# A transformer block with self- and cross-attention: the attention loop's instruction orders rewritten on five engines, and two tiles of cross keys placed by one group of transfers

## The chip, the cores and the metric

One core of a Trainium2 chip. The metric is the time of one execution on the device in microseconds (us), the median of several runs.

## What is computed

A batch of B = 32 items of N = 100 rows with D = 320 features passes a self-attention, a cross-attention to 361 context rows of 192 features, and a gated feed-forward layer, all in float32; both attentions have 20 heads of 16 features. Cut to what matters:

```python
def _attn(x, ctx, wq, wk, wv, wo, bo, heads):
    q, k, v = (heads_of(x @ wq), heads_of(ctx @ wk), heads_of(ctx @ wv))
    a = softmax(einsum('bhid,bhjd->bhij', q, k) * dh ** -0.5)
    return merge(einsum('bhij,bhjd->bhid', a, v)) @ wo + bo
h1 = _ln(x, n1_g, n1_b); x = _attn(h1, h1, q1, k1, v1, o1_w, o1_b, 20) + x
h2 = _ln(x, n2_g, n2_b); x = _attn(h2, context, q2, k2, v2, o2_w, o2_b, 20) + x
h3 = _ln(x, n3_g, n3_b); a, g = split(h3 @ ff_w1 + ff_b1)
return a * gelu(g) @ ff_w2 + ff_b2 + x
```

## The kernel before, in words

Three stages follow each other. A first stage makes the queries, keys and values of self-attention for all items and stores them in DRAM. The attention stage (`attention_phase`) is what the change touches. The feed-forward stage comes last.

The attention stage is a software pipeline without a loop in the program: for each engine an order of calls is written out by hand, `lead_in()`, 29 times `period(x, s, c, f)`, `run_out()`. In period p the roles are x = p, s = p + 1, c = p + 2, f = p + 3. Item f has its own (self-attention) scores made for their maximum, c goes through self-attention's exponentials and products, its output projection, the second norm, and the projections for cross-attention; s has its cross scores made for their maximum; x goes through cross-attention's exponentials and value products; y = x − 1 gets its cross output projection and its result. Every engine runs its calls strictly in the order written, and semaphores order the engines among each other. A call that has to wait holds back all calls behind it on its engine.

The steps, with the lines of the profile:

- `self_scores(f, i)` on TensorE (L167), two halves of ten matmuls, and `cross_scores(s, c)` (L785), ten pairs of matmuls of 362 columns, all write one PSUM tensor of two banks, `score`. So each of these twelve products waits (`empty_score`) until VectorE's `maximum` of the one before it (L174 for own, L1095 for cross scores) is done.
- `turn_max` (L796, job "MT1" or "MT2") transposes the finished maxima; ScalarE's `max_high` (L1392) and VectorE's `max_low` (L1111) split them into two parts of lower precision, and SyncE's `place_max` (L160) writes these into the query stack `qs`, as additional rows, so that the second product of queries and keys comes out with the maximum subtracted.
- `scores_for_exp` on TensorE (L811) makes that second product, two matmuls of 200 columns a tile, into two buffers `expin`; ScalarE's `exponential` (L1414) turns it into `probs`. There are 5 tiles for self-attention and 15 for cross-attention a period. `times_v` (L833) multiplies them with the values.
- `copy_product` (ScalarE, L181 and L183), `turn_heads` (VectorE, a transpose L1140 and a reciprocal L195), `scale_products` (GpSimd, L190), `turn_back` (VectorE, L1149), `heads_high` (ScalarE, L1435) and `heads_low` (GpSimd, L1628) bring the product into the form that `project_out` (TensorE, L702 and L705, eight matmuls) reads.
- `second_input` (VectorE, L1157) adds the residual, takes the statistics (L1161, L1164), and `normalise` (L1171) follows after GpSimd's `inverse_deviation`. `turn_normalised` (L684), `project_q2` (L702, L705) and `turn_q2` (L721) make the cross queries, which `copy_q2` and `q2_high` (ScalarE) and `q2_low` (VectorE) prepare. SyncE's `place_q2` (L566) writes them in six transfers into the stack, which GpSimd's `clear_cross` (L1603) has set to zero once the last exponent product of two items before has read it.
- `project_kc(c, t)` (L732 to L736, five matmuls, three tiles of keys) and `project_vc(c, i)` (L747 to L751, five matmuls, three tiles of values) project the context, which GpSimd splits into `ctx_hi` and `ctx_lo` (`split_first`, `split_last`, L1645 and L1646). `kc_high` (ScalarE, L1383) and `kc_low` (VectorE, L1111) prepare each key tile, and SyncE's `place_kc` (L548) writes it into the key stack `ks` in three transfers.
- All projections and transposes use three PSUM banks in turn, in the order of the list `WORK`: job number i goes to bank i mod 3, and waits until the job three before it has been read. `EXP` and `PV` number the exponentials and value products in the same way.

The seam of two periods on TensorE is this:

```python
cross_scores(s, 9)
turn_max(2, s)          # end of a period
self_scores(f, 0)       # next period, with the next f
```

Here `turn_max(2, s)` waits for the maximum of the pair just made.

## Time and profile before

| | us |
|---|---|
| median of 3 runs | 1479.38 |
| lowest, highest | 1477.76, 1483.56 |
| profiled execution | 1477.44 |
| its span, first to last instruction | 1475.5 |
| TensorE (matmuls) busy | 1317.4 |
| VectorE, ScalarE, GpSimd busy | 821.9, 675.6, 602.1 |
| mean granted clock of TensorE | 0.959 of full speed |

How to read the rows below: in a timeline a row gives start, duration, engine, line, operation, output and inputs, shapes and the number of instructions merged into it; in brackets stands the idle time just before it and what ended that. The modelled durations of successive matmuls overlap, so the time that a step takes of TensorE is read from its start to the next start. In a table of stretches a row gives the stretch and its length, then busy time and number of instructions for TensorE (matmuls), its weight loads, VectorE, ScalarE and GpSimd, then the granted clock (1.00 is 2.4 GHz, 0.50 is 1.2 GHz), the DMA share and GB/s. SPq is SyncE's queue; its durations are those of issuing transfers.

### The profile page before, as it was taken

How to read it: one execution, taken by the hardware profiler on the slowest of the kernel's cores; microseconds unless marked ns; L12 is line 12 of the kernel's file. 1: busy time of each engine (PE TensorE's matmuls, PEld its weight loads, DVE VectorE, ACT ScalarE, POOL GpSimd, SP SyncE). 2: the span in 40 equal slices, each digit the busy share in tenths (PEclk: the TensorE clock that was granted, in tenths of full speed). 3: DMA queues.
4: the chain of work that ended last, by engine and by line, in shares of the span. 5: the costliest groups of instructions: out<-in, count | busy, mean ns of one | idle time of the engine just before them, and what ended most of it. 6: DMA issues, size and time to landing. Idle time of an engine off the chain costs nothing. (4 is left out here: it accounts for less than half of the span.)

```text
span 1475.5 us, 34459 instructions
## 1 busy us (share of the span) xinstructions
PE 1317.4 (89%) x12788; PEld 1192.6 (81%) x12788; DVE 821.9 (56%) x1606; ACT 675.6 (46%) x1622; POOL 602.1 (41%) x792
## 2 busy tenths in 40 slices
PE   6898789988988898989889888988877999999999
PEld 5898678777777777777777777777657999999999
DVE  5464565766666666666666666667554524242421
ACT  5564244554555455455545554555444332323231
POOL 6331333444344444444443444344226533333341
PEclk9999889999999999999999999999888999999999
DMA  4677533443434444344434433342211110101000
GB/s 127 207 253 236 162 105 120 127 122 107 129 117 128 126 137 151 111 137 145 135 107 121 130 112 114 122 131 85 77 41 59 33 37 14 32 13 31 18 6 23
DMA packets 119691, 154.52 MB, mean 105 GB/s; under 512 B 23036, under 2 KB 113396, under 8 KB 119540
## 3 DMA queue, kind: packets, MB, share of 16 engines
q1 hardware_dynamic: 119540, 152.50, 33.5%
q8 instruction: 96, 1.57, 0.4%
q14 instruction: 55, 0.45, 0.1%
HBM read 62.98 MB, written 28.93 MB: 62 GB/s over the span
## 5 line engine op out<-in xcount | busy, mean ns | idle before, releaser
L1414 ACT ACTIVATE probs<-expin 120x400 f32<-120x400 f32 (+2 forms) x635 | 293.7, 504 | 242.9 <-PE expin L811 228.3
L1095 DVE TENSOR_REDUCE neg_max<-score 100x2 f32<-100x722 f32 x320 | 284.8, 890 | 78.6 <-PE score L785 78.6
L811 PE MATMUL expin<-qs,ks 128*120 128x200 f32 (+2 forms) x1270 | 233.7, 292 | 11.1 <-ACT probs L1414 8.9
L811 PEld LDWEIGHTS expin<-qs,ks 128*120 128x120 f32 (+2 forms) x1270 | 186.5, 189 | 49.8 <-ACT probs L1414 34.7
L785 PE MATMUL score<-ks,qs 128*100 128x362 f32 x640 | 172.8, 351 | 58.0 <-DVE neg_max L1095 55.1
L190 POOL TENSOR_TENSOR scaled_heads<-turned_heads,rden 128x320 f32<-128x320 f32 x63 | 47.7, 758 | 366.8 <-DVE rden L195 366.8
L785 PEld LDWEIGHTS score<-ks,qs 128*100 128x100 f32 x640 | 82.4, 166 | 97.1 <-issue 64.6
L2638 DVE SCALAR_TENSOR_TENSOR hidden<-ps_a,b_cols,gelu 128x320 f32<-128x320 f32 x100 | 55.0, 550 | 175.1 <-PE ps_a L2562 175.0
L174 DVE TENSOR_REDUCE neg_max<-score 100x10 f32<-100x1000 f32 x62 | 74.4, 1200 | 131.6 <-PE score L167 131.6
L2800 POOL TENSOR_TENSOR hid_lo<-hidden,hid_hi 128x320 fp32r<-128x320 f32 x100 | 88.0, 880 | 122.4 <-ACT hid_hi L2708 122.2
L1603 POOL MEMSET qs<- 128x2400 f32 (+1 forms) x58 | 112.6, 1941 | 32.9 <-PE expin L811 32.9
L2720 ACT ACTIVATE gelu<-ps_g,b_cols 128x320 f32<-128x320 f32 x100 | 52.8, 528 | 138.1 <-PE ps_g L2562 138.1
L2562 PE MATMUL ps_g<-t_hi,w_hi 128*128 128x320 f32 x300 | 92.6, 314 | 10.1 <-DVEq L2477 10.1
L833 PE MATMUL attn<-probs,vc 120*17 120x100 f32 (+1 forms) x3840 | 97.3, 251 | 0.1
L1111 DVE TENSOR_TENSOR kc_parts<-work,kc_parts 128x362 fp32r<-128x362 f32 (+1 forms) x96 | 51.0, 531 | 74.2 <-ACT kc_parts L1383 74.2
L2562 PE MATMUL ps_g<-t_hi,w_lo 128*128 128x320 f32 x300 | 91.8, 311 | 0.0
L2562 PE MATMUL ps_a<-t_hi,w_lo 128*128 128x320 f32 x300 | 91.6, 310 | 0.0
L2562 PE MATMUL ps_a<-t_hi,w_hi 128*128 128x320 f32 x300 | 91.5, 310 | 0.0
L833 PEld LDWEIGHTS attn<-probs,vc 120*17 120x17 f32 (+1 forms) x3840 | 80.8, 97 | 8.7 <-ACT probs L1414 1.1
L1628 POOL TENSOR_TENSOR t_lo_OT<-dense_heads,t_hi_OT 128x300 fp32r<-128x300 f32 x63 | 52.0, 825 | 77.1 <-ACT t_hi_OT L1435 77.1
L2579 PE MATMUL ps_y<-w_hi,hid_hi 128*128 128x320 f32 x250 | 78.5, 314 | 0.0
L2580 PE MATMUL ps_y<-w_lo,hid_hi 128*128 128x320 f32 x250 | 77.1, 309 | 0.0
(222 smaller groups left out, 3050.9 us busy)
## 6 DMA issues: line engine op xcount, KB each, us to landing
ks<-kc_parts SPq DMA_DIRECT2D x192, 181.0 KB, 2.7
qk_dram<-qk_parts SPq DMA_DIRECT2D x32, 500.0 KB, 5.3
qs<-q_parts SPq DMA_DIRECT2D x192, 75.0 KB
ks<-qk_dram SPq DMA_DIRECT2D x96, 125.0 KB
ctx_raw<-in_ctxT SPq DMA_DIRECT2D x64, 180.5 KB
ks<-kc_parts SPq DMA_DIRECT2D x96, 90.5 KB, 2.2
qs<-qk_dram SPq DMA_DIRECT2D x64, 125.0 KB
v_dram<-v_rows SPq DMA_DIRECT2D x32, 132.8 KB
```

The costliest lines, as they stand in the source:

```text
L174: return nc.vector.tensor_reduce(neg_max[:, :, n * i:n * (i + 1)], src, AX_X, ALU.max, negate=True)
L785: mm = pe.matmul(score[0:N, a, 0:JP], qs[2][u][:, a, q_slot(c), :], ks[2][u][:, c, :], start=True, stop=True)
L811: mm = pe.matmul(dst, ks[a][u][:, c, j0:j0 + n], qs[a][u][:, :, q_slot(c) if a == 2 else c, :], start=True, stop=True)
L833: mm = pe.matmul(attn[32 * i:32 * i + D1, g * N:(g + 1) * N], v, probs[EXP_AT[a, b, g, jt] % NPT][0:n, i * N:(i + 1) * N], start=(jt == 0) ...
L1095: ins = nc.vector.tensor_reduce(dst, src, AX_X, ALU.max, negate=True)
L1414: nc.scalar.activation(probs[e % NPT][0:n, :], expin[e % 2][0:n, 0:HG * N], ACT.Exp, scale=SCALE)\
L1603: link(nc.gpsimd.memset(stack.rearrange("p a c n -> p (a c n)").bitcast(F32), 0.0))
L2562: mm = pe.matmul(bank[:, 0:W], a, b, start=(k == 0), stop=(k == len(passes) - 1))
L2579: pe.matmul(y, hid_hi[:, f, c], w2_hi[:, f, :], start=(f == 0), stop=False)
L2580: pe.matmul(y, hid_hi[:, f, c], w2_lo[:, f, :], start=False, stop=False)
L2638: nc.vector.scalar_tensor_tensor(out=hidden[n % 2][:], in0=ps_a[n % 2][:, 0:W], scalar=b1[:, n % FT:n % FT + 1], in1=gelu[n % 2][:], op0=A ...
L2800: nc.gpsimd.tensor_tensor(hid_lo[:, f, c], hidden[n % 2][:], hid_hi[:, f, c].bitcast(F32), ALU.subtract).then_inc(hid_lo_made, 1)
```

## The change

It gives every engine a new order of calls in the attention stage, for the period, the lead-in and the run-out. The products still share one score buffer. Of the seam, `turn_max(2, ·)` moves into the next period, `project_vc(c, 0)` and `project_vc(c, 1)` move to the period's end, `project_vc(s, 2)` to the next period. The first exponent tile of an item's self-attention moves to the end of the period before. SyncE's `place_q2`, `place_max(2, ·)` and the placing of key tile 2 move over the seam as well, and so do GpSimd's context split, VectorE's `turn_back(2, ·)`, and others. `second_input` is parted into the residual and `statistics(b)`. Key tiles 0 and 1 are placed by one group of three transfers with rows twice as long, which needs another order of the ten key slots (`k_slot`); a period has six key transfers where it had nine. The lists `WORK` and `EXP` follow. The diff of the periods, of what they call, and of `work_jobs` and `exp_jobs`; the lead-in and the run-out follow the same new orders and are left out, apart from `project_out(2, 30)`, which in the run-out now stands between `turn_max(2, 31)` and `scores_for_exp(2, 31, 0, 0)`, and `project_out(1, 0)`, which comes after `self_scores(1, 0)`, `self_scores(1, 1)`, `turn_max(1, 1)` and two key projections; `load_qkv1(2)` is issued after `place_max(1, 1)` there.

```diff
 def work_jobs(x, s, c, f):
     y = None if x is None or x == 0 else x - 1
-    order = [("KC", c, 0), ("O2", y, 0), ("MT1", f, 0), ("KC", c, 1), ("O1", c, 0), ("KC", c, 2), ("VC", c, 0),
-             ("T2", c, 0), ("Q2", c, 0), ("VC", c, 1), ("QT", c, 0), ("VC", c, 2), ("MT2", s, 0)]
+    order = [("MT2", x, 0), ("VC", s, 2), ("O2", y, 0), ("MT1", f, 0), ("KC", c, 0), ("KC", c, 1), ("O1", c, 0),
+             ("T2", c, 0), ("KC", c, 2), ("Q2", c, 0), ("QT", c, 0), ("VC", c, 0), ("VC", c, 1)]
     return [job for job in order if job[1] is not None]
...
 def exp_jobs(x, s, c, f):
-    order = [(1, c, 0, 0), (1, c, 1, 0), (1, c, 2, 0), (1, c, 3, 0), (1, c, 4, 0), (2, x, 0, 0), (2, x, 0, 1),
-             (2, x, 0, 2), (2, x, 1, 0), (2, x, 1, 1), (2, x, 1, 2), (2, x, 2, 0), (2, x, 2, 1), (2, x, 2, 2),
-             (2, x, 3, 0), (2, x, 3, 1), (2, x, 3, 2), (2, x, 4, 0), (2, x, 4, 1), (2, x, 4, 2)]
+    order = [(1, c, 1, 0), (1, c, 2, 0), (1, c, 3, 0), (1, c, 4, 0), (2, x, 0, 0), (2, x, 0, 1), (2, x, 0, 2),
+             (2, x, 1, 0), (2, x, 1, 1), (2, x, 1, 2), (2, x, 2, 0), (2, x, 2, 1), (2, x, 2, 2), (2, x, 3, 0),
+             (2, x, 3, 1), (2, x, 3, 2), (2, x, 4, 0), (2, x, 4, 1), (2, x, 4, 2), (1, f, 0, 0)]
     return [job for job in order if job[1] is not None]
...
+
+
+def k_slot(c):
+    return 2 * (c % 4) + c // 4 if c < 8 else c
...
     def place_kc(b, t):
         u = b % 2
-        sp.wait_ge(*emptied(("KC", b, t)))
-        cross_stack_free(b, min(2 * t + 1, G - 1))
-        c0, n = KT[t]
+        for i in (0, 1) if t == 0 else (2,):
+            sp.wait_ge(*emptied(("KC", b, i)))
+        cross_stack_free(b, 3 if t == 0 else G - 1)
+        c0, n, tiles = (0, 8, slice(0, 2)) if t == 0 else (8, 2, slice(2, 3))
         for slot, part in ((0, 0), (1, 0), (2, 1)):
             sp.dma_start(ks[2][u][product_rows(slot), c0:c0 + n, :].bitcast(F32),
-                         kc_parts[0:32 * n, part, t, :].bitcast(F32)).then_inc(kc_landed[t][u], 16)
+                         kc_parts[0:32 * KT[t][1], part, tiles, :].bitcast(F32)).then_inc(kc_landed[t][u], 16)
...
     def period(x, s, c, f, e):
         y = x - 1 if x else None
-        load_x(f)
+        v = y - 1 if y else None
+        place_q2(s)
+        place_max(2, x)
         load_context(f)
-        place_kc(c, 0)
-        store_x2(y)
+        place_kc(s, 2)
+        load_x(e)
         place_max(1, f)
         load_qkv1(e)
-        place_q2(c)
-        place_max(2, s)
-        place_kc(c, 2)
-        place_kc(c, 1)
+        store_x2(v)
+        place_kc(c, 0)
...
-        if c % 4 == 0:
+        if c in (0, 8):
...
-            mm = pe.matmul(score[0:N, a, 0:JP], qs[2][u][:, a, q_slot(c), :], ks[2][u][:, c, :],
+            mm = pe.matmul(score[0:N, a, 0:JP], qs[2][u][:, a, q_slot(c), :], ks[2][u][:, k_slot(c), :],
...
     def period(x, s, c, f):
         y = x - 1 if x else None
         self_scores(f, 0)
-        scores_for_exp(1, c, 0, 0)
         scores_for_exp(1, c, 1, 0)
-        project_kc(c, 0)
         scores_for_exp(1, c, 2, 0)
+        turn_max(2, x)
+        project_vc(s, 2)
         scores_for_exp(1, c, 3, 0)
-        project_out(2, y)
+        scores_for_exp(1, c, 4, 0)
         self_scores(f, 1)
-        scores_for_exp(1, c, 4, 0)
         times_v(1, c, 0)
         times_v(1, c, 1)
         times_v(1, c, 2)
         times_v(1, c, 3)
         times_v(1, c, 4)
+        cross_scores(s, 0)
+        project_out(2, y)
+        turn_max(1, f)
         scores_for_exp(2, x, 0, 0)
-        cross_scores(s, 0)
+        cross_scores(s, 1)
         scores_for_exp(2, x, 0, 1)
-        turn_max(1, f)
+        project_kc(c, 0)
         scores_for_exp(2, x, 0, 2)
         scores_for_exp(2, x, 1, 0)
-        cross_scores(s, 1)
-        scores_for_exp(2, x, 1, 1)
-        times_v(2, x, 0)
-        scores_for_exp(2, x, 1, 2)
-        scores_for_exp(2, x, 2, 0)
         cross_scores(s, 2)
         project_kc(c, 1)
-        scores_for_exp(2, x, 2, 1)
-        scores_for_exp(2, x, 2, 2)
+        scores_for_exp(2, x, 1, 1)
+        scores_for_exp(2, x, 1, 2)
         cross_scores(s, 3)
         project_out(1, c)
+        scores_for_exp(2, x, 2, 0)
+        scores_for_exp(2, x, 2, 1)
+        cross_scores(s, 4)
+        times_v(2, x, 0)
+        scores_for_exp(2, x, 2, 2)
         scores_for_exp(2, x, 3, 0)
+        times_v(2, x, 1)
+        cross_scores(s, 5)
         scores_for_exp(2, x, 3, 1)
+        scores_for_exp(2, x, 3, 2)
+        turn_normalised(c)
         project_kc(c, 2)
-        cross_scores(s, 4)
-        scores_for_exp(2, x, 3, 2)
+        cross_scores(s, 6)
         scores_for_exp(2, x, 4, 0)
-        project_vc(c, 0)
+        project_q2(c)
+        cross_scores(s, 7)
         scores_for_exp(2, x, 4, 1)
-        cross_scores(s, 5)
         scores_for_exp(2, x, 4, 2)
-        turn_normalised(c)
-        times_v(2, x, 1)
         times_v(2, x, 2)
+        turn_q2(c)
+        cross_scores(s, 8)
+        scores_for_exp(1, f, 0, 0)
         times_v(2, x, 3)
         times_v(2, x, 4)
-        cross_scores(s, 6)
-        project_q2(c)
-        cross_scores(s, 7)
+        cross_scores(s, 9)
+        project_vc(c, 0)
         project_vc(c, 1)
-        turn_q2(c)
-        cross_scores(s, 8)
-        project_vc(c, 2)
-        cross_scores(s, 9)
-        turn_max(2, s)
...
-    def statistics():
+    def statistics(b):
+        dve.wait_ge(*emptied(("O1", b, 0)))
...
     def period(x, s, c, f):
         y = x - 1 if x else None
         maximum(1, f, 0)
+        max_low(2, x)
+        turn_back(2, y)
         maximum(1, f, 1)
-        kc_low(c, 0)
-        result(y)
         maximum(2, s, 0)
         turn_heads(1, c)
         maximum(2, s, 1)
-        max_low(1, f)
+        result(y)
         turn_back(1, c)
         maximum(2, s, 2)
+        max_low(1, f)
+        kc_low(c, 0)
         kc_low(c, 1)
+        maximum(2, s, 3)
         second_input(c)
-        maximum(2, s, 3)
+        statistics(c)
+        maximum(2, s, 4)
         normalise(c)
-        maximum(2, s, 4)
         maximum(2, s, 5)
         features_low("T2", c)
+        maximum(2, s, 6)
         kc_low(c, 2)
-        maximum(2, s, 6)
-        turn_heads(2, x)
         maximum(2, s, 7)
         maximum(2, s, 8)
         q2_low(c)
-        turn_back(2, x)
         maximum(2, s, 9)
-        max_low(2, s)
+        turn_heads(2, x)
     nc.vector.memset(attn[:, :], 0.0).then_inc(attn_cleared, 1)
...
     def period(x, s, c, f):
-        exponential(1, c, 0, 0)
+        y = x - 1 if x else None
+        copy_vc(s, 1)
+        copy_vc(s, 0)
         exponential(1, c, 1, 0)
         exponential(1, c, 2, 0)
+        max_high(2, x)
         exponential(1, c, 3, 0)
         exponential(1, c, 4, 0)
-        kc_high(c, 0)
+        heads_high(2, y)
+        copy_vc(s, 2)
         copy_product(1, c)
+        max_high(1, f)
         exponential(2, x, 0, 0)
         exponential(2, x, 0, 1)
-        max_high(1, f)
+        kc_high(c, 0)
         exponential(2, x, 0, 2)
         exponential(2, x, 1, 0)
+        heads_high(1, c)
+        kc_high(c, 1)
         exponential(2, x, 1, 1)
-        heads_high(1, c)
         exponential(2, x, 1, 2)
         exponential(2, x, 2, 0)
         exponential(2, x, 2, 1)
         exponential(2, x, 2, 2)
-        kc_high(c, 1)
         exponential(2, x, 3, 0)
         exponential(2, x, 3, 1)
+        features_high("T2", c)
         exponential(2, x, 3, 2)
+        kc_high(c, 2)
         exponential(2, x, 4, 0)
+        copy_q2(c)
         exponential(2, x, 4, 1)
-        features_high("T2", c)
         exponential(2, x, 4, 2)
-        kc_high(c, 2)
+        exponential(1, f, 0, 0)
+        q2_high(c)
         copy_product(2, x)
-        copy_vc(c, 0)
-        copy_q2(c)
-        copy_vc(c, 1)
-        q2_high(c)
-        heads_high(2, x)
-        max_high(2, s)
-        copy_vc(c, 2)
...
     lead_in()
     for p in PERIODS:
         x, s, c, f = roles(p)
+        y = x - 1 if x else None
+        e = p + 4 if p + 4 < B else None
+        scale_products(2, y)
+        split_first(c)
+        heads_low(2, y)
+        split_last(c)
         scale_products(1, c)
+        clear_own(e)
         heads_low(1, c)
-        clear_own(p + 4 if p + 4 < B else None)
         inverse_deviation(c)
         second_residual(c)
-        first_residual(f)
+        first_residual(e)
         clear_cross(c)
-        scale_products(2, x)
-        split_first(f)
-        heads_low(2, x)
-        split_last(f)
```

## Rows read from the trace of the kernel before

**Rows 1.** The page's busy times, TensorE, and its DMA issues, key transfers.
```profile
PE 1317.4 (89%) x12788; PEld 1192.6 (81%) x12788; DVE 821.9 (56%) x1606; ACT 675.6 (46%) x1622; POOL 602.1 (41%) x792
...
ks<-kc_parts SPq DMA_DIRECT2D x192, 181.0 KB, 2.7
```

**Rows 2.** Stretches: lead-in, loop, run-out, then two single periods of the loop.
```profile
150.29:192.24 41.95, 32.79 (x218) 27.33 (x218) 24.67 (x45) 11.72 (x30) 14.35 (x21) 0.87 0.51 156
...
192.24:1032.94 840.70, 744.45 (x8750) 648.48 (x8750) 552.27 (x927) 441.67 (x1101) 371.66 (x403) 0.96 0.40 122
...
1032.94:1104.80 71.86, 58.12 (x636) 47.20 (x636) 37.55 (x74) 33.04 (x79) 15.55 (x24) 0.85 0.22 60
...
540.28:568.40 28.12, 24.73 (x302) 21.41 (x303) 19.05 (x32) 15.23 (x38) 12.94 (x15) 1.00 0.45 137
...
568.40:598.06 29.66, 26.25 (x302) 22.93 (x303) 19.05 (x32) 15.24 (x38) 12.93 (x15) 0.94 0.42 130
```

**Rows 3.** Timeline of TensorE, one period at full clock: instructions that waited, waits in brackets.
```profile
542.27 0.41 PE L732 MATMUL work<-ctx_hi,w_c 128*128 128x362 f32 x1 [0.40 <-POOL ctx_lo L1646]
...
556.63 0.55 PE L785 MATMUL score<-ks,qs 128*100 128x362 f32 x2 [1.05 <-DVE neg_max L1095]
...
565.18 0.54 PE L785 MATMUL score<-ks,qs 128*100 128x362 f32 x2 [0.34 <-DVE neg_max L1095]
...
566.73 0.58 PE L785 MATMUL score<-ks,qs 128*100 128x362 f32 x2 [0.26 <-DVE neg_max L1095]
...
568.40 0.25 PE L796 MATMUL work<-identf,neg_max 100*24 100x100 f32 x1 [1.10 <-DVE neg_max L1095]
```

**Rows 4.** Timeline of TensorE, the same period: slots from start to start.
```profile
544.72 1.00 PE L167 MATMUL score<-ks,qs 128*100 128x100 f32 x10
...
545.56 0.39 PE L811 MATMUL expin<-qs,ks 128*100 128x200 f32 x2
...
545.87 1.05 PE L833 MATMUL attn<-probs,vs 100*17 100x100 f32 x40
...
546.86 0.46 PE L811 MATMUL expin<-qs,ks 128*120 128x200 f32 x2
...
547.15 0.50 PE L785 MATMUL score<-ks,qs 128*100 128x362 f32 x2
...
563.68 0.31 PE L747 MATMUL work<-w_c,ctx_hi 128*120 128x320 f32 x1
...
564.41 0.42 PE L721 MATMUL work<-identf,q_rows 100*128 100x100 f32 x3
```

**Rows 5.** Timeline of VectorE, the same period: a maximum of own scores, one of cross scores.
```profile
545.76 1.20 DVE L174 TENSOR_REDUCE neg_max<-score 100x10 f32<-100x1000 f32 x1 [3.06 <-PE score L167]
...
565.76 0.91 DVE L1095 TENSOR_REDUCE neg_max<-score 100x2 f32<-100x722 f32 x1 [0.72 <-PE score L785]
```

**Rows 6.** Stretches around the seam of two periods, and around a mid-period wait.
```profile
565.00:570.30 5.30, 3.45 (x24) 2.71 (x24) 3.46 (x7) 1.79 (x7) 4.35 (x6) 1.00 0.26 87
...
570.30:574.00 3.70, 3.62 (x15) 3.63 (x16) 0.53 (x1) 1.35 (x4) 0.00 (x0) 0.54 0.27 58
...
555.00:558.00 3.00, 1.95 (x14) 1.60 (x13) 2.74 (x6) 1.07 (x4) 2.15 (x4) 1.00 0.41 128
```

**Rows 7.** Timelines of the run-out: TensorE twice, GpSimd, SyncE's queue.
```profile
1053.82 0.46 PE L811 MATMUL expin<-qs,ks 128*121 128x200 f32 x2
...
1062.92 0.90 PE L785 MATMUL score<-ks,qs 128*100 128x362 f32 x2 [2.41 <-issue]
...
1054.34 2.10 POOL L1603 MEMSET qs<- 128x2400 f32 x1 [4.50 <-PE expin L811]
...
1056.58 4.84 SPq L566 DMA_DIRECT2D qs<-q_parts  x6
```

**Rows 8.** Timeline of TensorE, end of the run-out: maxima turned, first exponent product.
```profile
1081.10 0.25 PE L796 MATMUL work<-identf,neg_max 100*24 100x100 f32 x1
...
1084.89 0.67 PE L811 MATMUL expin<-qs,ks 128*120 128x200 f32 x4 [2.12 <-DMA qs<-max_parts]
```

More of the change, by code:

```diff
@@ L917, in run_out @@
                 cross_scores(30, 0)
+                project_out(2, 28)
                 scores_for_exp(2, 29, 0, 0)
@@ L1238, in lead_in @@
                 maximum(2, 0, 1)
+                turn_back(1, 1)
+                maximum(2, 0, 2)
+                max_low(1, 2)
+                kc_low(1, 0)
                 kc_low(1, 1)
-                maximum(2, 0, 2)
-                turn_back(1, 1)
                 maximum(2, 0, 3)
                 second_input(1)
+                statistics(1)
                 maximum(2, 0, 4)
```

282 lines of the change are left out of this document (144 added, 138 removed), and 17 rows, old and new, of tables (DRAIN_EXP, FILL_WORK).

## The prediction

> **What bounds the kernel now.** Read the page first: TensorE is busy 89% of the span, far ahead of every other engine [rows 1]. Then cut the span by stage [rows 2]: the 29 loop periods take 840.70 us of the 1475.5, at a mean granted clock of 0.96. So a period costs 28.99 us on average, but the one quoted at full clock took 28.12, and the next, with the same 302 matmuls, 29.66 at 0.94. Two losses follow. TensorE works 24.73 of the 28.12 us, so 3.4 us of every period is waiting; and the clock adds 840.70 − 29 × 28.12 = 25.2 us over the loop. VectorE works 19.05 us of a period, ScalarE 15.23: neither could set the end alone.
>
> The waits [rows 3] name their cause: 1.10, 1.05, 0.34 and 0.26 us for VectorE's maximum, because one score buffer serves all twelve score products, and 0.40 us for GpSimd's `ctx_lo`, which gates the first key projection. The 1.10 stands at the seam: `turn_max(2, s)` asks for the maximum of the product issued just before it, and the next period's `self_scores` sits behind it. Another small wait, for an exponential, makes up the rest.
>
> The clock falls at that seam. In the stretch before the fall the engine was busy 3.45 of 5.30 us, with the waits of 0.34, 0.26, 1.10 and 0.40 in it; then the clock was 0.54 (nearly all at its lower level, 1.2 GHz) for 3.7 us. Around the lone 1.05 wait in mid-period it stayed 1.00 [rows 6].
>
> **The change, part by part.** No instruction of TensorE, VectorE, ScalarE or GpSimd is added or dropped in a period; the order changes, so work is 24.73 us as before and only waits and clock can move. I walk TensorE's new order against VectorE's, with slots (start to next start) at full clock [rows 4]: half of the own scores 0.84, one exponent tile 0.30, five own value products 0.99, a value projection 0.73. That is 0.146 per matmul of 320 columns, so a projection of eight takes 1.17, a key projection (five of 362 columns) 0.83, a cross score pair (two of 362) 0.33, taken as 0.38; a cross value product of 24 I take as 0.6. The score buffer's cost [rows 5]: own scores from 544.72, maximum at 545.76 for 1.20, next score at 547.15, that is 1.04 + 1.20 + 0.19 = 2.43 start to start; cross pair 565.18, maximum 565.76 for 0.91, next pair 566.73, 1.55 to 1.6 start to start. Anything VectorE does in between adds if it lies in its way.
>
> *Seam.* Now `cross_scores(s, 9)` is followed by two value projections (1.46 us), and `turn_max(2, ·)` waits until after two exponent products of the next period. The maximum needs 1.6 us from the pair's start, the pair and the projections cover 1.85: the 1.10 goes. What is late next is `turn_heads(2, x)`, which now ends VectorE's period: 0.83 plus 0.3 behind that maximum, until about 0.6 us after the period's start, but the own scores' maximum can't start before 1.07. Covered.
>
> *Own scores.* Between the halves stand four exponent products, the turned maximum and `project_vc(s, 2)`: 0.9 + 1.2 + 0.13 + 0.73 = 3.0 us against 2.43. VectorE's `max_low(2, x)` and `turn_back(2, y)` end at about 3.2, before the second half's maximum can start (4.0). But between the second half (start 3.0) and `cross_scores(s, 0)` only the own value products stand, 0.84 + 0.99 = 1.8 us against 2.43. **A new wait of 0.6 us**, and its cover is nothing.
>
> *Cross scores.* Walking on, the ten pairs start at 5.4, 7.3, 9.4, 11.3, 13.4, 15.6, 17.8, 19.6, 21.5 and 23.3 us, and the buffer is free for them at 5.4, 7.0, 8.9, 11.0, 13.1, 15.1, 17.2, 19.4, 21.2 and 23.1 (VectorE's other steps counted where the new order puts them: `turn_heads` before pair 1's maximum, `result` and `turn_back` before pair 2's, both `kc_low` before pair 3's, residual and statistics before pair 4's, `normalise` before pair 5's). Nine margins of 0.2 to 0.6 us: the old 1.05, 0.34 and 0.26 go. The 0.40 goes as well, since `project_kc(c, 0)` now stands at 8.0 and the split ends at about 6.3 (own estimate: `split_first` starts when the two value projections are done and `scale_products(2, y)` has run, `heads_low` between). The walk ends at 25.2 us. Busy time plus the new wait gives 24.7 + 0.6 = 25.3; with 0.2 for margins that thin I take **25.5**. Ends: 24.9 (the new wait half covered) and 26.5 (0.1 us lost at each of the ten pairs on top).
>
> *Moved queues.* SyncE's nine key transfers of a period become six, three of them with twice the bytes. A 181 KB one lands in 2.7 us; twice that is at most 5.4 us, and `place_kc(c, 0)`, issued near 18, is read at 30.6: cost nothing, and without cover one landing. `place_max(2, x)` moves into the period that reads it. In the run-out 3.79 us passed from the turning to the first exponent product [rows 8]; now the turning ends at 1.6 and that product stands at 7.1: covered, by 1.7. `place_q2(s)` moves to the next period's head, and behind GpSimd's clearing of the stack. The run-out shows that chain bare [rows 7]: last exponent product of cross 1053.82, clearing 1054.34 for 2.10, six transfers from 1056.58 for 4.84, score at 1062.92: 9.1 us. In the walk it is 20.3 to 30.6, 10.3 us: covered by 1.2, the thinnest cover of the change. GpSimd and ScalarE keep their work; ScalarE's expensive neighbours, the exponentials, come 0.9 us apart on average against some 0.5 each. The own group-0 exponential a period earlier only needs `place_max(1, f)`, issued at about 11 for a reader at 22.
>
> *Clock.* Of the 3.4 us of waits 0.6 is left, in one place, shorter than the 1.05 after which nothing fell. I take all 25.2 us as regained; ends 0 and 25.2.
>
> *Lead-in and run-out.* 41.95 and 71.86 us [rows 2]. In the lead-in the first projection now comes after two own score halves (waits of about 3 us appear, and a later load of batch 2's keys costs 1.7), but the score chain behind it lacks the seam wait: −0.5, ends −3 and +3. In the run-out the chain of rows 7 starts 3 us earlier in its period, since no next batch's own scores stand ahead, and `project_out(2, 30)` fits under the 3.79 us: −4, ends −8 and +2.
>
> **Sum**, against the profiled execution (1477.44 us, span 1475.5; the median of the runs, 1479.38, is 1.9 higher): loop 29 × (28.12 − 25.5) = 76.0, clock 25.2, rest 4.5, together 105.7. 1477.4 − 105.7 = 1371.7, in median terms **1373**. A measurement here can tell about 0.5%, 7 us, from no change.
>
> **Rivals.**
> *The clock goes on falling* (22%). For it: the low stretches follow short waits, none over 1.10 us, and a wait a period remains. Against it: the lone 1.05 did nothing. With as many low stretches a period as now: 1373 + 25 = 1398; in proportion to the waits left (0.6 of 3.4) 1377. The Trainium skill (TensorE: Matmul & The Clock Gate, "A second HAM failure mode: psum-queue depth-cycling") says that an engine which idles briefly and often between groups, while it cycles through PSUM banks, swings between its clocks. By that rule the low stretches would stay; the trace agrees that such waits go before a fall, and does not show how few are harmless.
>
> *The score chain becomes the bound* (14%). All nine margins are under 0.6 us, so 0.3 us more on each handover (a step of VectorE in front of the maximum, an exponential ahead of a copy) uses most of them up: some 1.5 us a period, 1373 + 29 × 1.5 = 1416. For it: VectorE's 19.05 us now has to fit 25.5. Against it: the bare chain is 2 × 2.43 + 10 × 1.6 = 20.9 us, and much of the rest fits into the 0.6 us in which each pair is produced.
>
> *Slower: the query stack lands late* (4%). Place: `cross_scores(s, 0)` waits for `place_q2`, everything on TensorE behind it. With 9.1 us shown and 10.3 there, any longer chain costs its excess in all 29 periods; slower than before from 10.3 + (28.99 − 25.5) = 13.8 us on. Doubled key transfers just ahead in the queue could add at most the 2.7 above, which alone gives 11.8 and 1373 + 29 × 1.5; with the clearing 3 us late as well it is 14.8, 29 × 4.5 = 130 more, **1503**. Against it: clearing and transfers kept their times in every row seen.
>
> *It doesn't do what it says* (5%): some wait not in my walk takes the seam's place in full, so period and clock stay about as they are: 1475.
>
> **How the numbers follow.** Forecast 55%, clock 22%, score chain 14%, late stack 4%, no effect 5%. All but the last two are faster by far more than 0.5%: 0.91; half of "no effect" within 0.5%, with what lies between: 0.03; slower 0.06 (the late stack and the rest). Range: below, a 24.9 us period and the better ends of lead-in and run-out, 1373 − 17 − 5 = 1351; above, the clock rival and part of the score chain, 1416.
>
> **What would show it.** Right: first own-score maxima 25.3 to 25.7 us apart, evenly, with a granted clock of 1.00; one wait of about 0.6 us for `neg_max` ahead of `cross_scores(s, 0)`; none at the seam; no wait for a DMA on TensorE in the loop. Wrong, clock: spacing alternates as now. Wrong, chain: waits for `neg_max` of 0.2 or more ahead of most pairs. Wrong, stack: "DMA qs<-q_parts" as releaser of the first pair. A spacing over 26.5 us at full clock would refute the walk itself.

## The result, and the profile after

The kernel after takes **1336.55 us** (median of four runs, 1333.51 to 1341.66) against 1480.54 for the kernel before beside it: a ratio of 0.9031, 95% interval 0.8996 to 0.9065. The forecast was 1373 in a range of 1351 to 1416. The sign was right; the time lies 14 us below the low end of the range. The profiled execution took 1335.46 us.

The page of the kernel after, first the busy times, then TensorE's granted clock in 40 equal slices of the span in tenths, then the key transfers of two tiles at once (count, size, time to landing):

```profile
PE 1248.4 (94%) x12788; PEld 1168.4 (88%) x12788; DVE 826.6 (62%) x1606; ACT 672.8 (50%) x1622; POOL 602.7 (45%) x792
...
PEclk9999789999999999999999999998689999999999
...
ks<-kc_parts SPq DMA_DIRECT2D x96, 362.0 KB, 3.7
```

Beside [rows 1]: the other engines work as before, TensorE is booked 69 us less with the same 12788 matmuls. A key transfer of twice the size lands in 3.7 us, where two landings (5.4) had been the bound.

The stretches of the kernel after: lead-in, loop, run-out, one period at full clock.

```profile
150.14:199.21 49.07, 36.47 (x215) 32.37 (x216) 25.57 (x45) 11.02 (x28) 11.77 (x18) 0.74 0.45 137
199.21:891.02 691.81, 670.72 (x8751) 618.25 (x8751) 554.99 (x925) 438.88 (x1101) 371.56 (x402) 0.99 0.50 149
891.02:963.60 72.58, 59.04 (x641) 48.44 (x639) 38.64 (x76) 33.86 (x81) 18.96 (x27) 0.82 0.20 55
248.56:272.00 23.44, 23.04 (x305) 21.24 (x304) 19.16 (x33) 15.14 (x38) 12.97 (x15) 1.00 0.49 152
```

Against [rows 2] the loop is 148.9 us shorter (840.70 to 691.81), the lead-in 7.1 longer (41.95 to 49.07), the run-out 0.7 longer. The loop's first own score starts at 198.98 us, so the two figures with the cut at 199.21 are good to 0.2 us. A period at full clock went from 28.12 to 23.44 us: 2.99 us less waiting (3.39 to 0.40) and 1.69 us less "busy" (24.73 to 23.04). That second part was in no step of the forecast.

The period at full clock in TensorE's timeline, kernel after: both own score halves, the only wait, the last cross score pair, the next own scores.

```profile
248.62 1.00 PE L167 MATMUL score<-ks,qs 128*100 128x100 f32 x10
251.00 0.54 PE L786 MATMUL score<-ks,qs 128*100 128x362 f32 x2 [0.40 <-DVE neg_max L174]
...
267.70 0.58 PE L786 MATMUL score<-ks,qs 128*100 128x362 f32 x2
269.57 1.00 PE L167 MATMUL score<-ks,qs 128*100 128x100 f32 x10
```

The waits of [rows 3] are gone. One stands where the forecast put one, of 0.40 us where it said 0.6. At the seam 1.87 us pass from the last pair to the own scores, with two value projections between and no wait.

TensorE's waits over the whole loop, kernel after (us in total, times, longest):

```profile
PE score L786 <- DMA qs<-q_parts: 12.6, 9, 3.0
PE score L786 <- DVE neg_max L174: 8.0, 20, 0.4
```

The second row is the wait above. The first was not forecast for the likeliest case: in nine periods the cross queries land late. First own-score maxima are 23.41 to 23.47 us apart in 19 of 28 intervals, and 23.7 to 27.5 in the other nine, all around the ten in which SyncE also loads feed-forward weights. All 28 add up to 668.36 us, which is 28 × 23.44 = 656.3 and 12.0 more. Of these, 9.0 are the nine waits as far as they exceed the 0.40 that would have stood there anyway; the other 3.0 are what is left for two stretches of low clock, from 418 and from 589 us, each behind one of these waits (1.87 and 3.00 us). Behind a third one, longer than the first, the clock stayed at 1.00 (TensorE's timeline, kernel after):

```profile
466.86 0.54 PE L786 MATMUL score<-ks,qs 128*100 128x362 f32 x2 [2.07 <-DMA qs<-q_parts]
```

### The profile page after: what moved, and what is told of

Read it like the earlier page. It is cut to its first block and busy times, and to the rows that moved or that the text cites. A ratio compares the mean times of both kernels' runs of the same rounds, so it can differ in the third digit from the quotient of the medians.

```text
span 1333.7 us, 34303 instructions
## 1 busy us (share of the span) xinstructions
PE 1248.4 (94%) x12788; PEld 1168.4 (88%) x12788; DVE 826.6 (62%) x1606; ACT 672.8 (50%) x1622; POOL 602.7 (45%) x792
## 5 line engine op out<-in xcount | busy, mean ns | idle before, releaser
L1419 ACT ACTIVATE probs<-expin 120x400 f32<-120x400 f32 (+2 forms) x635 | 297.4, 506 | 133.1 <-PE expin L812 130.2
L1096 DVE TENSOR_REDUCE neg_max<-score 100x2 f32<-100x722 f32 x320 | 287.7, 899 | 105.9 <-PE score L786 104.7
L812 PE MATMUL expin<-qs,ks 128*120 128x200 f32 (+2 forms) x1270 | 201.4, 273 | 1.2 <-ACT probs L1419 0.9
L812 PEld LDWEIGHTS expin<-qs,ks 128*120 128x120 f32 (+2 forms) x1270 | 180.4, 183 | 11.3 <-ACT probs L1419 7.8
L786 PEld LDWEIGHTS score<-ks,qs 128*100 128x100 f32 x640 | 87.4, 168 | 50.0 <-issue 40.2
L834 PE MATMUL attn<-probs,vc 120*17 120x100 f32 (+1 forms) x3840 | 110.7, 255 | 0.0
L2597 PE MATMUL ps_y<-w_hi,hid_lo 128*128 128x320 f32 x250 | 77.1, 308 | 0.0
L167 PE MATMUL score<-ks,qs 128*100 128x100 f32 x620 | 64.3, 252 | 7.2 <-PEq L1765 5.9
```

The source lines that it names most:

```text
L786: mm = pe.matmul(score[0:N, a, 0:JP], qs[2][u][:, a, q_slot(c), :], ks[2][u][:, k_slot(c), :], start=True, stop=True)
L812: mm = pe.matmul(dst, ks[a][u][:, k_slot(c) if a == 2 else c, j0:j0 + n], qs[a][u][:, :, q_slot(c) if a == 2 else c, :], start=True, stop= ...
L834: mm = pe.matmul(attn[32 * i:32 * i + D1, g * N:(g + 1) * N], v, probs[EXP_AT[a, b, g, jt] % NPT][0:n, i * N:(i + 1) * N], start=(jt == 0) ...
L1096: ins = nc.vector.tensor_reduce(dst, src, AX_X, ALU.max, negate=True)
L1419: nc.scalar.activation(probs[e % NPT][0:n, :], expin[e % 2][0:n, 0:HG * N], ACT.Exp, scale=SCALE)\
L2597: mm = pe.matmul(y, hid_lo[:, f, c], w2_hi[:, f, :], start=False, stop=(f == FT - 1))
```

## The experiments

Ten kernels ran. Times are medians of four runs, or that of a single run where that is said; the kernel before took 1479.1 to 1484.4 beside them.

### The seam alone put back (e2)

```diff
-                cross_scores(s, 9)
                 project_vc(c, 0)
                 project_vc(c, 1)
+                cross_scores(s, 9)
```

> The kernel after, with only TensorE's order at the seam put back: in the period cross_scores(s, 9) comes after project_vc(c, 0) and project_vc(c, 1), so that the next self_scores stands right behind it and waits for its maximum. Theory (the seam's wait costs its own length, and short waits close together bring the clock down): 1.2 us of wait a period, 29 x 1.2 = 35 us, 1372, and where the clock falls after it, up to 1.5 us more for each fall, to 1395. Rival (the clock falls only after waits near 2 us, as at 416 and 588 us of the trace after): 1372 and no more clock falls than now. Second rival (the score chain has room and takes it up): under 15 us.

Measured: 1362.82 us, ratio 0.9184 (0.9155 to 0.9213). A period in the table of stretches, and around its seam:

```profile
251.68:276.43 24.75, 23.27 (x302) 21.18 (x303) 19.17 (x33) 15.13 (x38) 12.95 (x14) 1.00 0.48 143
246.50:251.68 5.18, 4.09 (x71) 3.52 (x68) 2.44 (x4) 2.42 (x7) 1.55 (x1) 1.00 0.64 224
251.68:256.62 4.94, 4.54 (x75) 4.28 (x75) 3.96 (x6) 2.89 (x8) 3.78 (x5) 1.00 0.19 65
```

And the seam wait in TensorE's timeline:

```profile
424.99 1.06 PE L167 MATMUL score<-ks,qs 128*100 128x100 f32 x10 [1.10 <-DVE neg_max L1096]
```

The old wait of 1.10 is back in every period, and costs 24.75 − 23.44 = 1.31 us: 1.10 shown as a wait, and 0.21 to 0.23 in "busy" time (23.27 against 23.04). **This wait costs some 0.2 us more than it shows**, most of it in the slot just ahead of it: the second matmul of the last pair takes 0.32 us there, where 0.17 is usual. Over 29 periods 1.31 makes 38 us, but the whole is only 26 us slower than the kernel after (35 were expected), because with a longer period the cross queries are late in four periods instead of nine (2.3 us of waits for them in place of 12.6). And the clock stays at 1.00 on both sides of the wait, in all 28 periods. So the falls of the kernel before did not come from a wait of 1.10 us by itself, as far as the new order can tell.

### Two waits close together (e5)

As above, and both halves of the own scores next to each other:

```diff
                 self_scores(f, 0)
+                self_scores(f, 1)
                 scores_for_exp(1, c, 1, 0)
...
                 scores_for_exp(1, c, 4, 0)
-                self_scores(f, 1)
```

> The kernel of e2_seam_back, and on TensorE self_scores(f, 1) right behind self_scores(f, 0), so that a wait of 1.1 us at the seam is followed 0.9 us later by one of about 1.5 us for the own scores' maximum; the wait of 0.40 ahead of cross_scores(s, 0) goes. e2 had a wait of 1.1 and one of 0.4 in each period, 3.8 us apart, and no clock fall. Theory (the clock falls where waits stand close together, as 0.34, 0.26, 1.10 and 0.40 within 5 us did before): falls come back in a third to all of the periods, 1.5 us or more each, spacing of the own-score maxima 25.9 at full clock and over 27.4 with a fall, loop over 765 us. Rival (what brought the clock down before was something other than the waits' crowding, a single wait has to reach about 2 us): all periods 25.9, loop 751 us.

Measured: 1433.51 us, one run; every period 27.35 us. Around one seam, in TensorE's timeline and in the table of stretches:

```profile
417.23 1.06 PE L167 MATMUL score<-ks,qs 128*100 128x100 f32 x10 [1.09 <-DVE neg_max L1096]
419.58 1.08 PE L167 MATMUL score<-ks,qs 128*100 128x100 f32 x10 [1.29 <-DVE neg_max L174]
```

```profile
412.20:417.23 5.03, 3.94 (x67) 3.37 (x67) 2.44 (x4) 2.28 (x6) 1.40 (x1) 1.00 0.69 241
417.23:420.50 3.27, 1.98 (x20) 1.85 (x21) 2.09 (x3) 0.00 (x0) 2.19 (x3) 1.00 0.16 54
420.50:424.50 4.00, 4.00 (x52) 3.81 (x55) 1.75 (x3) 2.45 (x7) 0.81 (x2) 0.57 0.03 7
```

One more wait of 1.29 us right behind the one of 1.09, and the clock falls in every period, for some 4 us at 0.57. The 2.60 us over e2's period come out by an estimate: the new wait costs 1.29 + 0.21, the one of 0.40 it displaces gave back 0.61, and 4.0 us at 0.57 instead of 1.00 are 1.7 us of work. So the forecast read [rows 6] rightly in this: the clock falls behind waits of 1.09 and 1.29 us that stand 1.06 us apart, and does not behind a lone one of 1.10 us.

What decides a fall is not settled by that. In the kernel before, the waits at a seam (0.34 to 0.36, then 0.26 to 0.28, then 1.10 us, and 0.3 to 0.4 us behind them where the clock is still up) are the same at each of the 28 seams inside the loop, and a stretch of low clock begins at 14 of them. Here is one where none does, with the first row of [rows 3] right behind it, in TensorE's timeline of the kernel before:

```profile
540.28 0.25 PE L796 MATMUL work<-identf,neg_max 100*24 100x100 f32 x1 [1.10 <-DVE neg_max L1095]
```

And in the kernel after, single waits of 1.87 and 3.00 us were followed by a fall, one of 2.07 us was not.

### Exponentials over a quarter of a tile, before (e4) and after (e4b)

```diff
-nc.scalar.activation(probs[e % NPT][0:n, :], expin[e % 2][0:n, 0:HG * N], ACT.Exp, scale=SCALE)
+nc.scalar.activation(probs[e % NPT][0:n, 0:N], expin[e % 2][0:n, 0:N], ACT.Exp, scale=SCALE)
```

> The kernel before, with each exponential taken over a quarter of its tile (100 of 400 columns; the value products read that quarter for all four heads), so this leaves three quarters of the exponentials out. Theory (TensorE's 24.73 us busy in a full-clock period hid waits for exponentials, since a row of merged or overlapping matmuls shows a wait only in part): busy time of a period falls by 0.5 to 0.8 us to about 24.1 at the same count of matmuls, while the wait of 1.05 for the maximum grows by about as much and the period stays within 0.7 us of 28.1. Rival (the matmuls themselves take that long in the old neighbourhood, and the new order made them cheaper): busy stays at 24.7.

> The kernel after, with every exponential in the attention loop over a quarter of its tile; three quarters of the exponentials are left out. Control for the same edit in the kernel before, where it took 0.43 us off a period. Theory, the new walk leaves TensorE no hidden wait for ScalarE: the period stays at 23.44 us with 23.0 us busy, and the run stays within 4 us of 1336. Rival, the new walk hides such waits as well: the period falls by over 0.3 us and the run by over 9 us, and then the gain of the change in the busy time is something else.

Both leave three quarters of the exponentials out. One run each; e4 took 1458.44 us (before beside it 1484.4). A period at full clock, first of e4, then of e4b:

```profile
533.90:561.55 27.65, 24.48 (x303) 21.50 (x303) 19.04 (x32) 10.75 (x38) 12.93 (x15) 1.00 0.46 140
```

```profile
247.80:271.23 23.43, 23.03 (x310) 21.25 (x306) 18.96 (x33) 10.54 (x39) 12.95 (x15) 1.00 0.50 148
```

Before, the short exponentials take 28.12 to 27.65 us: 0.22 of it in shown waiting (3.39 to 3.17), 0.25 in "busy" (24.73 to 24.48). That is half of the least that the theory gave for "busy" (0.5), and the wait of 1.05 did not grow as expected. After, the same edit changes nothing in the period (23.44, 23.04). So the old order made TensorE wait for ScalarE, half of it unseen, and the new one does not. The whole e4b took 1325.76 us, 11 under the kernel after where at most 4 were expected. Hardly any of it lies in the loop; from the turned maxima of the last item to the last output projection it takes 951.36 − 931.33 = 20.0 us, in the kernel after 961.24 − 936.25 = 25.0: 5 of the 11 us there alone. The last item's exponent products do wait for exponentials there, but the five shown waits are of 0.19 us each; the larger difference is the granted clock, 0.50 from 941 to 957 us in the kernel after, 1.00 from 938 to 951 us in e4b. That the waits brought it down is likely and not shown.

### Keys placed in nine transfers again (e3)

```diff
+                for i in (0, 1) if t == 0 else (2,):
+                    c0, n = KT[i]
                     for slot, part in ((0, 0), (1, 0), (2, 1)):
...
-    return 2 * (c % 4) + c // 4 if c < 8 else c
+    return c
```

> The kernel after, with key tiles 0 and 1 placed by three transfers each again (nine key transfers a period, ten slots in their old order), the rest as it is. Theory (SyncE's queue is off the path in most periods; in those with the feed-forward weights it is just late): 0 in the 19 other periods, 0 to 1.9 us in the ten with weights, so 1336 to 1355. Rival (the merged group is what makes the order possible, since place_q2 must start right after the clearing and three more issues of 0.63 us push it back by 1.9 us everywhere): 1.5 us or more in each period, 1380 or more.

Measured: 1360.47 us, ratio 0.9169 (0.9141 to 0.9197), 24 us slower than the kernel after. Waits of the loop, and SyncE's queue in a period without weights:

```profile
PE score L787 <- DMA qs<-q_parts: 36.5, 18, 4.0
```

```profile
306.59 3.89 SPq L551 DMA_DIRECT2D ks<-kc_parts  x6
```

Six issues take 3.89 us where three take 1.9. In most periods without weights that hurts nobody, and the period is 23.44 us here too. But not in all: of the 18 waits for the queries, three of over 0.5 us (0.54, 1.74 and 0.62) stand before the first weights, which are asked for at 408 us, and two (1.10 and 0.99) some 200 us after the last. GpSimd's clearing, SyncE's queue and TensorE around the longest of them:

```profile
355.33 2.10 POOL L1611 MEMSET qs<- 128x2400 f32 x1 [3.13 <-PE expin L813]
...
355.20 5.47 SPq L551 DMA_DIRECT2D ks<-kc_parts  x6
360.78 3.74 SPq L569 DMA_DIRECT2D qs<-q_parts  x6
...
366.01 0.54 PE L787 MATMUL score<-ks,qs 128*100 128x362 f32 x2 [1.74 <-DMA qs<-q_parts]
```

The six key issues took 5.47 us, so the queries were asked for 3.35 us after the clearing, and the clock fell behind the wait. From the loop's first own-score maximum to its last this kernel needs 701.15 us, 32.8 more than the kernel after; its lead-in is 3.8 us shorter. Of what it needs above 23.44 a period, 4.6 us lie in the periods before the weights and well behind them, and nearly all the rest in and behind the periods with weights (24.5 to 29.5 us). So the grouping is worth little where no weights are loaded, and most of its 24 us once they stand between the keys and the queries. The expected 1355 at most was passed by 5 us; the rival's 1380 was not reached.

### The feed-forward weights elsewhere (e1, e6)

The kernel after issues two weight transfers (256 and 128 KB) at the end of each of ten periods, between the keys and the queries. GpSimd's clearing, SyncE's queue and TensorE, kernel after, first a period without weights, then the first with them:

```profile
311.97 2.11 POOL L1610 MEMSET qs<- 128x2400 f32 x1 [3.13 <-PE expin L812]
...
314.35 4.58 SPq L568 DMA_DIRECT2D qs<-q_parts  x6
...
321.32 0.55 PE L786 MATMUL score<-ks,qs 128*100 128x362 f32 x2 [0.40 <-DVE neg_max L174]
```

```profile
405.75 2.10 POOL L1610 MEMSET qs<- 128x2400 f32 x1 [3.14 <-PE expin L812]
...
407.10 1.09 SPq L643 DMA_DIRECT2D w_raw<-in_ff_w  x1
408.24 0.71 SPq L644 DMA_DIRECT2D w_raw<-in_ff_w  x1
409.06 4.21 SPq L568 DMA_DIRECT2D qs<-q_parts  x6
...
416.57 0.55 PE L786 MATMUL score<-ks,qs 128*100 128x362 f32 x2 [1.87 <-DMA qs<-q_parts]
```

Without weights the queries are asked for 0.3 us after the clearing and land in time. With them they are asked for 1.2 us after it (0.3 to 2.0 us in the ten periods), and the last lands 416.57 − 413.27 = 3.3 us after the end of issuing, behind 384 KB of weights.

e1 moves the whole load behind `load_x(e)`, into mid-period; e6 parts it into 20 transfers, one in each of 20 periods, right behind the queries and maxima:

```diff
                 place_q2(s)
                 place_max(2, x)
+                if 4 <= p < 4 + 2 * FF // P:
+                    load_w1((p - 4) // 2, p % 2)
                 load_context(f)
...
-                if 8 <= p < 8 + FF // P:
-                    load_w1(p - 8)
```

> The kernel after, with load_w1 of periods 8 to 17 issued in mid-period (behind load_x(e), where SyncE's queue stands idle) instead of just ahead of place_q2. Theory (the feed-forward weights' transfers lie ahead of the query stack's in the rings and make them land late): the nine waits for qs<-q_parts of 12.6 us in the loop shrink to the 0.40 for the maximum that every other period has, the two clock falls that follow the longest of them go too, all loop periods are 23.44 us, and the time falls by 12 us to about 1324. Rival (the chain from the last exponent product over GpSimd's clearing is too long by itself in these periods): the waits stay, 1336. Second rival: the weights now delay place_max(1, f) or load_qkv1(e) and a wait of 1 us or more appears elsewhere, 1330 to 1345.

> The kernel after, with the 20 transfers of the feed-forward weights issued one a period (periods 4 to 23) right behind place_max(2, x), where SyncE's queue waits for the context split anyway. e1 moved both of a period to behind load_x(e) and gained half of what was expected; there they pushed place_max(1, f), load_qkv1(e) and with them place_kc(c, 0) back by 2 us, so that 1.1 MB of keys lay in the rings just ahead of place_q2. Theory: here nothing behind is pushed back, no wait for qs<-q_parts in the loop (at most 1 us in total), all periods 23.44, loop 680 us, time 1324 (12 less than after). Rival (the weights' bytes in the rings anywhere in the period are enough to make the query stack late): waits of 0.5 us or more in ten or more periods, 1330 or more.

Measured: e1 1327.90 us where 1324 was expected, ratio 0.8939 (0.8898 to 0.8979), with 5.3 us of waits for the queries left in four periods; e6 **1319.93 us**, ratio 0.8907 (0.8868 to 0.8946), every period but two 23.44 us (23.54 and 23.83), one such wait of 0.5 us, loop 680.30 us. In e1 the weights pushed everything behind them on SyncE's queue back. In each of its four periods with a wait the key transfers were issued right ahead of the queries, and these were asked for 0.6 to 1.3 us after the clearing; here it is 0.63 (kernel e1: clearing, SyncE's queue, TensorE):

```profile
574.57 2.10 POOL L1610 MEMSET qs<- 128x2400 f32 x1 [3.12 <-PE expin L812]
...
575.25 1.94 SPq L550 DMA_DIRECT2D ks<-kc_parts  x3
577.30 5.25 SPq L568 DMA_DIRECT2D qs<-q_parts  x6
...
584.39 0.54 PE L786 MATMUL score<-ks,qs 128*100 128x362 f32 x2 [0.88 <-DMA qs<-q_parts]
```

The 12 us lost in the kernel after were thus the weights' place. e6 gained 16.6 us by the medians and 13.9 between the profiled executions, 11.5 of them in the loop; what the rest is stays open, and part of it can be scatter (the four runs of the kernel after span 8 us).

### The lead-in (e7), and all together (e8, e9)

e7 gives the lead-in an order near the old one on every engine; TensorE's:

```diff
+                project_out(1, 0)
                 self_scores(1, 0)
-                self_scores(1, 1)
-                turn_max(1, 1)
                 project_kc(0, 0)
                 project_kc(0, 1)
-                project_out(1, 0)
+                self_scores(1, 1)
                 turn_normalised(0)
                 project_kc(0, 2)
                 project_q2(0)
+                turn_max(1, 1)
```

On SyncE `load_qkv1(2)` and `place_kc(0, 0)` move ahead of `place_max(1, 1)`. e8 is e6 and e7 together with this in the run-out (and VectorE's `result(30)` behind `turn_heads(2, 31)`):

```diff
                 turn_max(2, 31)
-                project_out(2, 30)
                 scores_for_exp(2, 31, 0, 0)
...
                 times_v(2, 31, 4)
+                project_out(2, 30)
```

e9 is e8 with one line moved on SyncE:

```diff
                 load_qkv1(2)
+                place_max(1, 1)
                 load_x(2)
                 place_kc(0, 0)
-                place_max(1, 1)
                 place_q2(0)
```

> The kernel after, with the first half of the lead-in in nearly the order of the kernel before: project_out(1, 0) first on TensorE, then own scores and key projections in turn, load_qkv1(2) before place_max(1, 1) on SyncE's queue, and the other engines to match. Theory (the lead-in's 49 us against 42 before come from the waits of 1.29, 1.29, 3.27 and 0.90 us, which stand one behind the other, and from the clock at its lower level until about 169 us): lead-in 43 to 45 us, time 5 us less, 1331. Rival (the wait for batch 0's query stack behind load_qkv1(2) and the score chain of the second half set its end): less than 2 us.

> e6 and e7 together, and in the run-out project_out(2, 30) back behind times_v(2, 31, 4), with result(30) to match on VectorE. Theory: gains add, 12 + 5 and 1 to 2 for the run-out's wait of 2.67 us, which only partly lies under the landing of the last maxima: 1318. Rival (run-out sets no end): 1320; or, where the gains overlap, 1325.

> As the run with all three edits, but with place_max(1,1) asked for ahead of the second query stack's load on SyncE's queue (order: load_qkv1(2), place_max(1,1), load_x(2), place_kc(0,0), place_q2(0)). Theory, the order of requests on the queue sets when the maxima's parts land: they land about 2.4 us earlier, the wait of 6.08 us for them at 167 us shrinks to some 3.7 us, the lead-in is 43.7 us long and the run takes 1316 us. Rival, the keys and queries that are now asked for later become the late ones: the wait moves to them and the time stays at 1318 us. Loop and run-out stay (679.9 us from the first own score to the last).

Measured: e7 1330.93 us, ratio 0.8971 (0.8926 to 0.9017), lead-in 45.7 us against 49.1 (its ratio's interval overlaps that of the kernel after, so the whole gain of 5.6 us is not clear of scatter); e8 **1318.19 us**, ratio 0.8899 (0.8863 to 0.8935); e9 1320.64 us, ratio 0.8929 (0.8914 to 0.8943). TensorE in the lead-in and the stretch behind the wait, kernel e8, then the same of kernel e9:

```profile
167.19 0.66 PE L814 MATMUL expin<-qs,ks 128*100 128x200 f32 x2 [6.08 <-DMA qs<-max_parts]
```

```profile
170.00:175.00 5.00, 4.59 (x64) 4.01 (x62) 1.93 (x3) 2.71 (x7) 1.30 (x2) 0.81 0.13 37
175.00:180.00 5.00, 3.50 (x18) 2.91 (x19) 4.82 (x9) 1.60 (x4) 1.58 (x2) 1.00 0.43 108
```

```profile
165.84 0.63 PE L814 MATMUL expin<-qs,ks 128*100 128x200 f32 x2 [1.95 <-DMA qs<-max_parts]
```

```profile
170.00:175.00 5.00, 4.51 (x56) 4.06 (x55) 1.20 (x1) 1.93 (x5) 1.38 (x3) 0.50 0.38 112
175.00:180.00 5.00, 4.16 (x16) 3.57 (x16) 3.64 (x6) 1.04 (x4) 0.80 (x2) 0.54 0.46 118
```

e9's wait is 4.1 us shorter, and the lead-in as long (150.66 to 196.32 us, e8: 148.96 to 194.48). The time went into the clock: from 170 to 180 us e9 runs near its lower level, e8 largely at the higher. A wait of 0.49 us for the queries came with it. The rival was right that the time stays, but mostly for a reason that neither side of e9's expectation had; why the clock stayed low there is not shown. In the run-out the moved output projection did let the exponent products start 4.0 us after the turned maxima instead of 4.5, no more: another wait, of 3.79 us for the maxima's landing, stood behind it. e8 and e6 can't be told apart (their intervals overlap), so what e8's two further edits bring together is within the noise. The best version is e6 or e8, some 17 us below the kernel after.

## Why the prediction was wrong, point by point

**What failed: "TensorE works 24.73 of the 28.12 us" and "work is 24.73 us as before".** The forecast took busy time for work. The end of a matmul is modelled in the profile, and the slot of an instruction that stands ahead of a wait holds part of that wait: e2 shows it (0.32 us for the matmul ahead of the wait, 0.17 for its like elsewhere). The measured period has 23.04 us of "busy", not 24.73. Here are TensorE's slots of a period at full clock, start to next start less the waits shown, added up by kind from the timelines of both kernels:

```
us                          before   after
exponent tiles (20)           5.38    4.48
turnings and transposes       1.17    0.54
last matmul of kc, vc         1.35    0.92
cross score pairs (10)        3.92    3.70
own scores (20 matmuls)       1.73    1.77
value products (20 tiles)     3.83    4.14
```

The same instructions, 1.8 us less in these rows (the kinds left out differ by 0.1 the other way, which gives the 1.69). Two causes can be priced from runs. The unseen part of waiting for exponentials is 0.25 (e4). Four other shown waits went (1.10, 1.05, 0.34 and 0.26); with the 0.21 that e2 measured on the first of them taken for each, that is 0.84, an estimate. The other 0.6 is not assigned, and its cause stays open.

**The second failure is the price of 0.30 for an exponent tile.** It came from two tiles of [rows 4] that stand singly ahead of another kind of product. Slots of one tile in that same period go from 0.19 to 0.40, 5.38 / 20 = 0.27 in the mean. Here are two tiles in a row, timeline of the kernel after:

```profile
524.22 0.57 PE L812 MATMUL expin<-qs,ks 128*120 128x200 f32 x4
524.63 0.44 PE L685 MATMUL work<-identf,z 100*128 100x100 f32 x3
```

That is 0.41 us for two, and over a period 4.48 / 20 = 0.22 each. Twenty tiles at 0.30 put 1.5 us too much into the walk of 25.2, which is nearly all of its error against 23.44; the new wait (0.40 for 0.6) makes 0.2 more, and smaller errors of the other slots nearly cancel. The walk and "busy time plus the new wait", 25.3, agreed by chance, each too high by about 1.8 us, one through the tile's price, the other through old waits inside the busy time, and I took the agreement for a confirmation. Then 0.3 us of caution went on top: 25.5.

The terms, against the profiled execution:

```
term                       forecast   measured
period, 29 x               -76.0      -135.7   (28.12 - 23.44 = 4.68 each)
clock, loop unevenness     -25.2       -13.2   (12.0 of the 25.2 lost again)
lead-in                     -0.5        +7.1
run-out                     -4.0        +0.7
rest of the execution        0          -0.9
sum                       -105.7      -142.0
```

**Seam: right.** The 1.10 went, and nothing of `turn_heads(2, x)` showed up in its place. Put back alone (e2) it costs 1362.8 − 1336.6 = 26 us, or 38 by the length of a clean period; either way not the largest part of 142.

**New wait: right** in place and cause, 0.40 for 0.6.

**Cross scores: right that the margins hold**, and the score chain rival is refuted: ten pairs, no wait for `neg_max` of a cross pair in a clean period, although VectorE's 19.16 us now stand in 23.44.

**Clock: right that nearly all comes back.** The rival that the clock goes on falling is refuted in the kernel after (0.99 over the loop, 20 shown waits of 0.40) and more strongly by e2, which waits 1.10 and 0.40 us in every period at 1.00. The rule weighed in the forecast is that of the Trainium skill (TensorE: Matmul & The Clock Gate, "A second HAM failure mode: psum-queue depth-cycling"), by which brief idle times that come often make the engine swing between its clocks. It agrees with the kernel before (a fall at 14 of 28 seams) and with e5 (one in every period), where the waits stand together, and not with the kernel after or e2, where a wait or two a period left the clock at 1.00. "I take all 25.2 us as regained" failed through the late queries, which cost 9.0 in waits and 3.0 in clock. The mechanism in the forecast, that short waits close together bring the clock down, holds in e5, but it does not say which of like clusters do.

**`place_q2`, "the thinnest cover of the change": right as a warning, with the wrong threat.** The forecast bounded what could lengthen the chain by the doubled keys, and didn't count `load_w1`, which stands between key and query transfers in ten periods. A shorter period also took cover away. The doubled keys were no threat but a help: without the grouping it is 24 us worse (e3), which the forecast had costed at nothing.

**Lead-in: wrong by 7.6 us**, past its worse end of +3. It named waits of "about 3 us". By [rows 2] and the stretches above, 3.4 of the 7.1 us are more waiting (9.16 to 12.60) and 3.7 more busy time with nearly the same matmuls at a granted clock of 0.74 instead of 0.87; the second part had no term in the forecast. TensorE's timeline there, and the first ten us, kernel after:

```profile
153.31 1.91 PE L167 MATMUL score<-ks,qs 128*100 128x100 f32 x10 [1.29 <-DVE neg_max L174]
156.51 0.34 PE L797 MATMUL work<-identf,neg_max 100*20 100x100 f32 x1 [1.29 <-DVE neg_max L174]
...
165.33 0.72 PE L685 MATMUL work<-identf,z 100*128 100x100 f32 x3 [3.27 <-DVE z L1173]
```

```profile
150.00:155.00 5.00, 3.56 (x20) 3.43 (x20) 2.16 (x5) 0.00 (x0) 0.80 (x3) 0.50 0.53 158
155.00:160.00 5.00, 3.71 (x15) 3.52 (x15) 1.99 (x3) 0.74 (x3) 0.87 (x1) 0.50 0.22 68
```

The kernel before was at 1.00 from 155 to 160 us. e7, with the old kind of order, got 3.4 of the 7.1 us back in the length of the lead-in, by less waiting (9.8 us) and not by the clock (0.72).

**Run-out: wrong by 4.7 us.** The chain of [rows 7] did start earlier: the last item's first cross score pair comes 25.4 us after the loop's end instead of 30.0, more than the 3 us forecast. But `project_out(2, 30)` did not "fit under the 3.79 us". TensorE, kernel after:

```profile
936.25 0.25 PE L797 MATMUL work<-identf,neg_max 100*24 100x100 f32 x1 [1.10 <-DVE neg_max L1096]
939.17 0.95 PE L703 MATMUL work<-w_o,t_hi_OT 128*100 128x320 f32 x5 [2.67 <-ACT t_hi_OT L1440]
```

It waited 2.67 us for heads that ScalarE hadn't split, and the exponent products stood behind it. The stretches from there on (4.5 and 20.5 us against 3.79 and 17.75) took back most of what had been won, the second at a granted clock of 0.58 against 0.71; the cross score pairs ahead of them took 19.8 us against 18.2.

Two small slips of the forecast's sums change nothing: 1371.7 and the 1.9 of the medians make 1373.6, not 1373, and the better ends of lead-in and run-out are 2.5 and 4 us from their terms, so the low end would be some 1350. The measured 1336.55 lies below that too.

## What to carry to other kernels

Before you call busy time work, look for the waits in it: price an instruction by the mean of its slots over a period and not by two of them, and try some 0.2 us more than a shown wait says for its removal (one wait was measured, at 1.31 for 1.10). When waits go, ask where the next ones cluster: two of 1.09 and 1.29 us with 1.06 us between them cost a fall of the clock in every period, a single one of 1.10 us none. When a load is moved to a place with 1 us of cover, list every transfer that can stand ahead of it on its queue, the ones of other stages too: in the kernel after, moving the weights gave 11.5 us back in the loop.

## What was unexpected in the hardware

A wait of 1.10 us costs 1.31 (e2), the difference being booked as busy. A transfer of 362 KB lands in 3.7 us where one of 181 KB takes 2.7. The same waits at the seam went with a fall of the clock at 14 of 28 seams of the kernel before, and single waits of 1.87 and 3.00 us were in the kernel after where one of 2.07 us was not. In the lead-in a wait of 6.08 us, cut to 1.95, gave nothing back, as the clock was lower (0.69 over the lead-in against 0.80; e9, e8).
